# Layer 1 rotary embedding: ScalarE copies the halves exchanged, VectorE multiplies by the cosine, GpSimd by the sine, in new orders within a head

## What is computed

```python
x1, x2 = (x[..., :d2], x[..., d2:])                       # d2 = 64
rot = concatenate([x1 * cos - x2 * sin, x2 * cos + x1 * sin], axis=-1)
q, k = rot(q), rot(k)
attn = einsum('bhqd,bhkd->bhqk', q, k) * scale            # masked to the window
out = einsum('bhqk,bhkd->bhqd', softmax(attn), v)
return out.reshape(...) @ wo
```

## Time and profile before

| | |
|---|---|
| runs | 687.96, 692.9, 690.5 us (median 690.5) |
| profiled execution | 684.86 us, of which the span of instructions 683.3 us |
| granted TensorE clock, mean | 0.995 |
| TensorE busy | 642.0 us |
| VectorE busy | 529.0 us |
| ScalarE busy | 346.2 us |
| GpSimd busy | 335.5 us |
| layer 1, heads 0 to 13 | from 199 to 482 us of the span |

### The profile page before, as it was taken

One profiled execution on the slowest core, in us unless ns is written; L12 is line 12 of the kernel. 1 busy time (PEld: TensorE's weight loads), 2 busy tenths in 40 slices (PEclk: granted clock), 3 DMA queues, 4 the chain that ended last, 5 costly groups with the idle time before them and its releaser, 6 DMA issues.

```text
span 683.3 us, 13489 instructions
## 1 busy us (share of the span) xinstructions
PE 642.0 (94%) x4844; PEld 504.5 (74%) x4844; DVE 529.0 (77%) x1068; ACT 346.2 (51%) x752; POOL 335.5 (49%) x267
## 2 busy tenths in 40 slices
PE   3998999999899999999999999989989998899987
PEld 1445778788478988888898787878968746657766
DVE  4278876698698998988899998576437879689994
ACT  1497212300556485755647565465454663279441
POOL 1053555592457677474857736898238432120000
PEclk9999999999999999999999999999999999999999
DMA  8801000000601001010100102102321200100001
GB/s 250 347 1 63 2 2 1 1 1 0 239 17 40 25 8 38 19 42 16 38 23 8 38 16 57 46 22 61 139 68 44 58 1 0 39 0 1 1 1 62
DMA packets 14647, 31.37 MB, mean 46 GB/s; under 512 B 1837, under 2 KB 8587, under 8 KB 14029
## 3 DMA queue, kind: packets, MB, share of 16 engines
q1 hardware_dynamic: 12813, 26.46, 11.8%
q0 software_dynamic: 1536, 3.15, 1.8%
q10 hardware_dynamic: 256, 1.18, 0.6%
HBM read 26.59 MB, written 5.24 MB: 47 GB/s over the span
## 4 chain that ended last, share of the span: by engine, by line
PE 53%; DVE 17%; issue 11%; ACT 10%; POOL 4%; DMA 3%; SPq 0%; DVEq 0%; POOLq 0%; ACTq 0%
PE bank L613 9%; PE bank L614 7%; PE bank L615 7%; PE bank L603 6%; PE bank L594 6%; PE bank L806 3%; DVE arena L1740 2%; PE bank L836 2%; DVE arena L1739 2%; PE bank L820 2%; PE bank L835 2%; DMA arena<-in_lA 2%; DVE x L1765 2%; DVE arena L1749 1%; PE bank L709 1%
## 5 line engine op out<-in xcount | busy, mean ns | idle before, releaser
L613 PE MATMUL bank<-zone 128*128 128x256 f32 (+1 forms) x472 | 167.4, 355 | 11.2 <-DVE arena L1740 3.0
L614 PE MATMUL bank<-zone 128*128 128x256 f32 (+1 forms) x472 | 156.6, 332 | 0.0
L615 PE MATMUL bank<-zone 128*128 128x256 f32 (+1 forms) x472 | 156.4, 331 | 0.0
L613 PEld LDWEIGHTS bank<-zone 128*128 128x128 f32 x472 | 88.9, 188 | 36.8 <-issue 12.2
L2209 POOL TENSOR_TENSOR arena<-arena 128x512 f32<-128x512 f32 x64 | 82.2, 1284 | 61.2 <-ACT arena L1317 61.2
L615 PEld LDWEIGHTS bank<-zone 128*128 128x128 f32 x472 | 89.1, 189 | 9.1
L2214 POOL TENSOR_TENSOR arena<-arena 128x512 f32<-128x512 f32 x64 | 83.1, 1298 | 24.3 <-DVE arena L1740 13.6
L614 PEld LDWEIGHTS bank<-zone 128*128 128x128 f32 x472 | 89.2, 189 | 5.2
L1336 ACT ACTIVATE arena<-arena 128x256 f32<-128x256 f32 (+1 forms) x128 | 62.1, 487 | 29.4 <-DVE arena L1749 28.8
L1749 DVE CUSTOM_DVE_ANT_0 arena<-bank,const 128x256 f32<-128x256 f32 (+1 forms) x128 | 45.7, 403 | 23.6 <-PE bank L806 22.2
L1765 DVE SCALAR_TENSOR_TENSOR x<-bank,arena,x 128x256 f32<-128x256 f32 x128 | 53.0, 473 | 9.2 <-PE bank L615 8.5
(11 more groups left out here) (298 smaller groups left out, 1331.4 us busy)
## 6 DMA issues: line engine op xcount, KB each, us to landing
arena<-in_qk SPq DMA_DIRECT2D x16, 256.0 KB, 2.7
arena<-in_tern SPq DMA_DIRECT2D x1, 3072.0 KB, 22.4
arena<-in_wv SPq DMA_DIRECT2D x8, 256.0 KB, 2.9
arena<-in_wo SPq DMA_DIRECT2D x16, 128.0 KB, 2.1
arena<-in_wr SPq DMA_DIRECT2D x1, 1792.0 KB, 9.3
lB<-in_lB SPq DMA_DIRECT2D x1, 1288.5 KB, 24.9
x<-in_x SPq DMA_DIRECT2D x2, 512.0 KB, 8.0
xg_rows<-arena SPq DMA_DIRECT2D x1, 1024.0 KB
```

The source lines that it names most:

```text
L613: pe.matmul(dst, lhi, rhi, start=(n == 0), stop=False)
L614: pe.matmul(dst, lhi, rlo, start=False, stop=False)
L615: last = pe.matmul(dst, llo, rhi, start=False, stop=(n == len(terms) - 1 and not open_end))
```

## The change

ScalarE no longer copies the bank as it is. It makes two copies of 64 partitions each, and each goes to the other half of the tile (now `qturn`). VectorE makes one product of 128 partitions, the bank with the cosine (`qcos`), and raises `rope_half` as before. GpSimd multiplies `qturn` by the sine and adds `qcos`. The sine's sign changes side in the constants. Besides, three orders change: on ScalarE the last two copies of transposed probabilities come together, and output block 0 and the rounding of the next weights go ahead of the copy of tile 3; on VectorE the rotation of tile 3 goes behind the residue of output block 0; on GpSimd `rest_of_wqk` goes ahead of the rotation of tile 3.

```diff
@@ scalar block
-                act.activation(qraw[:, j, :], ps[j % 2], ACT.Copy).then_inc(raw_kept, 1)
+                act.activation(qturn[0:64, j, :], ps[j % 2][64:128, :], ACT.Copy)
+                act.activation(qturn[64:128, j, :], ps[j % 2][0:64, :], ACT.Copy).then_inc(raw_kept, 1)
...
                 if more:
                     keep_raw(h + 1, 2)
                 keep_pT(h, 2, base)
+                keep_pT(h, 3, base)
+                keep_oT(h, 0, base)
+                if more_v:
+                    round_wqk(h + 2)
                 if more:
                     keep_raw(h + 1, 3)
-                keep_oT(h, 0, base)
-                keep_pT(h, 3, base)
                 keep_oT(h, 1, base)
                 if more_v:
-                    round_wqk(h + 2)
                     if c:
                         keep_v(pair + 1)
@@ vector block
-                dve.tensor_tensor(qsin[0:64, j, :], ps[j % 2][64:128, :], sinT[64:128, at], ALU.mult)
-                dve.tensor_tensor(qsin[64:128, j, :], ps[j % 2][0:64, :], sinT[0:64, at], ALU.mult).then_inc(rope_half, 1)
+                dve.tensor_tensor(qcos[:, j, :], ps[j % 2], cosT[:, at], ALU.mult).then_inc(rope_half, 1)
...
                 if more:
                     rotate(h + 1, 2)
-                    rotate(h + 1, 3)
...
                 for b in range(NB):
                     rest_of_oT(h, b)
+                    if more and b == 0:
+                        rotate(h + 1, 3)
@@ gpsimd block
-                    pool.tensor_tensor(qraw[:, j, :], qraw[:, j, :], cosT[:, at], ALU.mult).then_inc(cos_done, 1)
-                    pool.wait_ge(cos_done, h * 4 + (j + 1))
+                    pool.tensor_tensor(qturn[:, j, :], qturn[:, j, :], sinT[:, at], ALU.mult).then_inc(sin_done, 1)
+                    pool.wait_ge(sin_done, h * 4 + (j + 1))
...
-                    pool.tensor_tensor((kT1, qT1)[j % 2][:, at], qraw[:, j, :], qsin[:, j, :], ALU.add).then_inc(qk_ready, 1)
+                    pool.tensor_tensor((kT1, qT1)[j % 2][:, at], qturn[:, j, :], qcos[:, j, :], ALU.add).then_inc(qk_ready, 1)
...
                 rest_of_wo(h)
-                turn_qk(h + 1, (2, 3), base)
+                turn_qk(h + 1, (2,), base)
+                rest_of_wqk(h + 2)
+                turn_qk(h + 1, (3,), base)
```

More of the change, by code:

```diff
@@ L233, in build @@
         affT_ready = sem("affT_ready")
-        xT1_kept, cos_done = sem("xT1_kept"), sem("cos_done")
+        xT1_kept, sin_done = sem("xT1_kept"), sem("sin_done")
         xT_hi, wqk_hi, wqk_split, wo_hi, wo_split, raw_kept, oT1_hi = (
@@ L323, in build @@
         qT1, kT1, v1 = m.cols(T), m.cols(T), m.grid(NT, 2 * DH)
-        qsin = m.grid(4, BW)
+        qcos = m.grid(4, BW)
         S1_at = m.at
@@ L344, in build @@
         assert y.at <= m.at
-        qraw = m.grid(4, BW)
+        qturn = m.grid(4, BW)
         xg = xT.rearrange("p k t -> p (k t)").rearrange("p (t d) -> p t d", t=NT)
@@ L2253, in _ @@
                     beside_head(i * 2 + c)
-                    rest_of_wqk(i * 2 + (c + 2))
                     if c == 0:
@@ L2264, in _ @@
                 beside_head(h, between=lambda: send_rows(later))
-                rest_of_wqk(h + 2)
                 if h % 2 == 0:
@@ L2366 @@
     freq = np.arange(T, dtype=f32)[None, :] * inv[:, None]
-    cossin = np.concatenate([np.tile(np.cos(freq), (2, 1)), np.concatenate([np.sin(freq), -np.sin(freq)], 0)], 1).astype(f32)
+    cossin = np.concatenate([np.tile(np.cos(freq), (2, 1)), np.concatenate([-np.sin(freq), np.sin(freq)], 0)], 1).astype(f32)
     rst = np.tile((np.arange(T) % CH != 0).astype(f32), (P, 1))
```

## The result

The change made the kernel slower: 694.3 us (median of 17 runs, 692.3 to 695.8) against 690.5 us for the kernel before in its 17 runs (688.0 to 692.9). The ratio is 1.0053, 95% interval 1.0041 to 1.0066, so +3.7 us, where the forecast was 687.9 us and its range ended at 693.0 us.

A forecast was written before the change was run, and what follows sets the result against it. The prediction took TensorE, busy 642.0 of 683.3 us, as the bound, so only its waits count. Terms of -0.2 - 1.3 - 0.6 - 0.4 - 0.3 + 0.2 = -2.6 us took 690.5 to 687.9 us, range 684.0 to 693.0.

The forecast's parts named there:

- Step of ScalarE's halves: ScalarE's rotary copies: halves start 0.48 us apart, so each bank's copy ends 0.48 us later; 31 us more ScalarE work, mostly hidden.
- rival B: ScalarE's halves don't overlap (step 0.59 us), enlarging the new wait and delaying the weights: +1.8, 692.3 us; chance 0.14.
- rival C: ScalarE's halves take 0.69 us, losing 1.53 us in every head that opens a pass: about +10, 700 us; chance 0.06.
- Cover at the transposed weights: Transposed weights behind the second bank's copy end at 324.97, TensorE wants them at about 324.96; nothing counted.
- Rotation wait: TensorE's wait before the projection at 323.68 for VectorE's late rotation: gain 0.22 us in each head opening a pass.
- Residue and weight wait: TensorE's waits for VectorE's first output residue (0.14 us) and GpSimd's weight residue (0.22 us) per pair: both gone.
- New wait before output projection 1: In each head that opens a pass, TensorE waits 0.25 us because VectorE's second residue comes late.
- The pair of heads: Heads 0 to 7, four pairs, each -0.22 - 0.14 - 0.22 + 0.25 us: -1.3 us together.
- Heads 8 to 13: Gains of -0.6 us in heads 8 and 9, -0.4 in head 10, -0.3 in heads 11 to 13.
- Head 14: The second residue is 0.2 us late, with VectorE's remainder of the head behind it: +0.2 us.
- Start of the layer: Two of four waits for a rotated bank get 0.22 us shorter, less a small loss: -0.2 us.
- rival D: At the layer's start, GpSimd's later rotations delay VectorE's routing comparisons: +0.3 instead of -0.2, 688.4 us; chance 0.15.

The follow-up runs named there:

- the better kernel: The kernel before with GpSimd's new order and VectorE's tile 3 pair between the two output residues, ScalarE's order old: 682.8 us, ratio 0.9960.

## Why the prediction was wrong

The reading of the bound held: TensorE sets the time, and only its waits count. Step by step:

- **Step of ScalarE's halves: the term that failed.** I took 0.48 us from the earlier trace rows, "the row of the same engine", and bounded it by 0.59, "if halves on different partitions do not overlap". It is 0.61, and the hold also falls on the first half and on the operation behind the second. A bank's copy costs 0.86 us more than before where ScalarE has no pause, where the forecast said 0.48 and rival B 0.59. The upper bound left out the two neighbours. The row that showed it was at hand: VectorE's pair of halves in the earlier trace rows does not overlap at all (1.38 for two, against 1.24 for two whole residues), and I kept it for rival C alone.
- **Cover at the transposed weights: "just used up; I count nothing".** Two copies of 0.38 us more than counted make the weights 0.76 late, and TensorE waits 0.80 us in head 6 and 0.6 to 1.0 in the even heads from 2 to 12 and in head 9. This one place is most of the loss in the nine heads. Rival C's price for it, 0.8 us, is what was measured, though C took the halves for slower than they are. A cover of 0.01 us should have had a price for each further tenth; even at steps of 0.48, 0.27 us is lost there.
- **Rotation wait, -0.22 in even heads: wrong.** The bank was to be free 0.22 us sooner. Counted from the exponential in front, the second half ends 0.75 us later than the whole copy did, and VectorE gives back 0.70. So 0.26 us are lost at 326.69, 0.04 more than before.
- **Residue and weight wait, -0.14 and -0.22 a pair: right**, both gone.
- **New wait before output projection 1, +0.25: right in kind**, 0.34 measured (0.23 in the profile with two whole copies).
- The pair of heads: forecast -0.33; by the rows of head 6 +0.04 - 0.14 - 0.22 + 0.34 + 0.80 = +0.82; by the marks +0.9 in each of three pairs and +0.35 in the first, where the wait for the weights is missing.
- **Heads 8 to 13: -1.3 was forecast, +2.7 measured in the first pair of profiles**, 1.1 of it in head 8 and 1.6 in heads 9 to 13 (marks of heads 9 and 14, 4.97 and 6.58 us late). This second number is not firm: heads 9 to 13 take 103.5, 105.0 and 107.0 us in the three profiles of before and 105.1, 105.0 and 105.4 in those of after, with low clock in some. The weights' 2.14 us wait is gone as forecast; in the first profile of after 0.9 us of it comes back in the next projections. But the halves are late here too, in all three: TensorE loses 1.0 us at the transposed weights in head 9 and 0.6 to 0.8 in heads 10 and 12.
- **Head 14, +0.2: not contradicted.** The first profiles differ by -1.3 there, and 1.5 of it is the low clock of before at 506 us, which leaves +0.2; the second pair differs by +0.8, the third by -0.2.
- **Start of the layer, -0.2; rival D, +0.3.** The mark of head 0 is 0.8 us late, but it moves by 1 to 2 us between profiles of one kernel. Counted from it, the comparisons end 0.3 to 0.4 us later in the kernel after, and TensorE loses 0.33 to 0.38 us behind them, as rival D priced it; the kernel with the new arithmetic in the old orders shows the delay too, the one with the old arithmetic in the new orders does not. Whether a shared port does it was not tested.
- **The last head was not in the sum.** It has no rotation, but ScalarE's output copy 0 now stands behind the transposed weights 3. TensorE's wait before its output projection 1 is 1.40 us instead of 0.80 in undisturbed profiles, and two of 0.4 precede it: 1.4 us together. A stretch of low clock, between 581 and 590 us, follows in all five profiles that have the new ScalarE order and no late row maximum (the second of after, the new orders alone, two whole copies, and the two that move the halves). Of the six such profiles with the old order it follows only in the first of before; why is open. From the mark of head 15 to the end the five take 161.3 to 162.2 us; with the old order the second profile of before, the new arithmetic in old orders, GpSimd's order alone and the better kernel take 158.3. That is **3 us that no term of the sum held**, and they belong to ScalarE's order and not to the halves.
- **Rival B was the right mechanism, too cheap and given 0.14.** It priced the step only, +1.8 us, 692.3. With 0.76 us at the transposed weights in its seven heads the forecast's sum becomes -2.6 + 5.3 = +2.7, the sign and most of the size. On the chip where before took 686 us the change costs 7 us. Of the difference between the second profiles of the two kernels 4.1 us lie in the nine heads and 3.1 behind the mark of head 15.

Kernel before, second profile, the last head's projection, and the kernel after, second profile:

```profile
538.24 0.38 PE L613 MATMUL bank<-zone 128*128 128x256 f32 x1 [0.80 <-DVE zone L1756]
```
```profile
546.40 0.38 PE L613 MATMUL bank<-zone 128*128 128x256 f32 x1 [1.40 <-DVE zone L1757]
```

What the experiments did not settle: why two whole copies gain only 0.5 us over nine heads where my steps said 1.3 (0.27 of it a pair is the wait at the transposed weights).

## What to carry to other kernels

Splitting an operation by partitions to exchange halves costs three things, not one: the second operation, the overlap between the two, and the overlap with both neighbours. Price it as whole durations laid end to end, on ScalarE and VectorE alike. Before a cost is booked at nothing, compare the slack in the waiting engine's start with the error of the estimate, and walk the queue behind the operation until something absorbs it: moving the halves out of the way only moved the wait. Look at what a change does in parts: of the orders that were made for the new arithmetic, GpSimd's was worth 2.3 us on the old one, and ScalarE's cost about 6 (1.0045 with it, 0.9960 without). And follow a new order into the last head, where other work stands around it: 3 us of this change lay there, and the sum had no term for them.

## What the hardware showed unexpectedly

- ScalarE holds an instruction back when the first partition of its source or its destination differs from that of the one before: 0.60 to 0.61 us from start to start instead of 0.48, for 512 columns; alone, with nothing else running, just as in the kernel. A copy of 64 partitions takes as long as one of 128.
- TensorE's clock falls to 1.2 GHz for 3.4 us behind some waits of 0.6 to 2.2 us, in one execution at one place and in the next at another. At 1.5 us each, and 0 to 3 of them in a profile, this is as large as the effect measured here.
- One kernel's median was 685.5 to 686.3 us on some chips and 689.7 to 690.5 on others, and the ratio of two kernels moved with it from 1.0105 to 1.0024. Marks inside the profile that lie away from those waits agreed to 0.1 us.
